# Two graph layers on one core: the table's scatters two rounds later, and the third graph sorted before its lists are made

## The reference

```python
scores = where(A != 0, -arange(N), -inf); vals, idx = top_k(scores, 25)
agg = X[idx].max(axis=2)                       # (N, 256) per graph
agg = where(degree <= 25, maximum(agg, 0), agg)
x1 = layernorm(X + relu(concat([X, agg]) @ W0 + b0))
Wh = x1 @ W1                                   # 8 heads of 32
e = leaky(s1[:, None] + s2[None, :] + edge_emb[1])   # per head
h = softmax(where(A == 0, -1e9, e)) @ Wh
out = layernorm(x1 + elu(layernorm(h) * gamma + beta))
```

## Time and profile before

| | before |
|---|---|
| median of three runs | 3414.9 us (3408.55 to 3415.16) |
| the profiled execution: its time | 3413.55 us |
| the profiled execution: its span | 3411.9 us |
| GpSimd (POOL) busy | 2487.7 us, 73% |
| VectorE (DVE) busy | 2417.1 us, 71% |
| TensorE (PE) busy | 1586.7 us, 47% |
| ScalarE (ACT) busy | 1113.9 us, 33% |
| DMA, mean over the span | 179 GB/s |

### The profile page before, as it was taken

The page is one execution under the profiler, slowest core; times in us unless marked ns, Lnnn a source line. Parts: engine busy times, 40 slices in busy tenths (PEclk is TensorE's granted clock), DMA queues, the critical chain, the costliest instruction groups (busy, mean ns, idle before and its releaser), DMA issues.

```text
span 3411.9 us, 25547 instructions
## 1 busy us (share of the span) xinstructions
PE 1586.7 (47%) x5123; PEld 1178.9 (35%) x5131; DVE 2417.1 (71%) x5791; ACT 1113.9 (33%) x2307; POOL 2487.7 (73%) x2612
## 2 busy tenths in 40 slices
PE   0036355444555344643555345554555434566454
PEld 0024233333343233432333233343334323344342
DVE  8798787667776668867786778767786455566666
ACT  3224343323333234342443334222332212223234
POOL 2476777777777777777777777777777777777775
PEclk9976667766666666766667666666667666667776
DMA  6657776655656566675666666555544444444332
GB/s 234 213 195 235 256 273 198 214 183 190 202 194 225 169 202 195 212 232 176 213 208 203 216 189 217 167 182 152 166 131 115 124 114 116 117 119 117 108 106 72
DMA packets 221587, 610.01 MB, mean 179 GB/s; under 512 B 68849, under 2 KB 112882, under 8 KB 194802
## 3 DMA queue, kind: packets, MB, share of 16 engines
q0 software_dynamic: 122880, 342.62, 33.8%
q1 hardware_dynamic: 98546, 265.71, 22.8%
HBM read 555.19 MB, written 52.95 MB: 178 GB/s over the span
## 4 chain that ended last, share of the span: by engine, by line
POOL 66%; issue 22%; DVE 7%; DMA 1%; DVEq 1%; ACT 1%; PE 1%; SPq 0%; POOLq 0%; ACTq 0%
POOL ring L590 57%; POOL sorted_d L567 4%; POOL out_dram L616 4%; DVE cand L1022 2%; DVE agg L1145 2%; POOL table_d L609 1%; DVEq L983 1%; POOL pair_s L600 1%; DVE adj_h L1018 1%; DMA adj_i<-in_adj_dram 0%; DVE lists L1006 0%; DMA ring<-sorted_d,idx_cur 0%; PE lin_p L844 0%; DVE agg L1135 0%; DMA pair_s<-sorted_d,pair_cur 0%
## 5 line engine op out<-in xcount | busy, mean ns | idle before, releaser
L590 POOL DMA_INDIRECT ring<-table_d,idx_loc x1096 | 1047.6, 956 | 333.9 <-issue 333.3
L590 POOL DMA_INDIRECT ring<-sorted_d,idx_cur x685 | 659.5, 963 | 208.7 <-issue 208.4
L852 PE MATMUL score_p<-ident,x1k 128*128 128x128 f32 x256 | 81.3, 419 | 1411.8 <-ACT x_t L690 1407.9
L880 PE MATMUL att_p<-ring,ident 128*128 128x256 f32 (+1 forms) x2384 | 602.4, 411 | 138.6 <-DVE ring L1302 138.0
L1145 DVE TENSOR_REDUCE agg<-ring 128x256 f32<-128x2560 f32 (+9 forms) x120 | 453.5, 3779 | 267.9 <-DMA ring<-sorted_d,idx_cur 183.6
L880 PEld LDWEIGHTS att_p<-ring,ident 128*128 128x128 f32 (+1 forms) x2384 | 497.4, 210 | 242.0 <-DVE ring L1302 126.7
L852 PEld LDWEIGHTS score_p<-ident,x1k 128*128 128x128 f32 x256 | 35.9, 197 | 1461.1 <-issue 1456.4
L721 ACT ACTIVATE neg<-z 128x256 f32<-128x256 f32 x128 | 53.3, 416 | 1466.9 <-DVE z L1188 1466.9
L590 POOL DMA_INDIRECT ring<-in_x_dram,idx_cur x411 | 395.3, 962 | 130.8 <-issue 124.3
L844 PE MATMUL lin_p<-w_s,h_t 128*128 128x256 f32 x1024 | 475.3, 645 | 0.0
L844 PEld LDWEIGHTS lin_p<-w_s,h_t 128*128 128x128 f32 x1024 | 319.9, 327 | 149.0 <-issue 80.9
(11 more groups left out here) (159 smaller groups left out, 2733.8 us busy)
## 6 DMA issues: line engine op xcount, KB each, us to landing
adj_i<-in_adj_dram SPq DMA_DIRECT2D x208, 1024.0 KB, 5.5
ring<-table_d,idx_loc POOLq DMA_INDIRECT x1096, 2.8
pay<-in_x_dram SPq DMA_DIRECT2D x8, 2048.0 KB, 9.9
xs<-sorted_d SPq DMA_DIRECT2D x128, 128.0 KB, 5.6
ring<-sorted_d,idx_cur POOLq DMA_INDIRECT x685
table_d<-tab SPq DMA_DIRECT2D x80, 132.0 KB, 3.9
ring<-in_x_dram,idx_cur POOLq DMA_INDIRECT x411
sorted_d<-pay,rank_i POOLq DMA_INDIRECT x128, 2.7
```

The source lines that it names most:

```text
L590: pool.indirect_dma_start(out=to[:, k * width:(k + 1) * width], out_offset=None, in_=source, in_offset=bass.IndirectOffsetOnAxis(ap=idx_at ...
L880: last = pe.matmul(att_p[:, 0:C], ident[0:on, :], r3[0:on, s, 0:C], start=(s == 0), stop=(s == k - 1))
```

## The change

`LAG0` goes from 7 to 9: the table's tile i is scattered in round i + 9, but at the latest in round 23 after its graph's first, so tiles 14 and 15 both come there, just ahead of the first gather of the graph's table. `RANKED` goes from 3 to 2: graph 2 is treated as graphs 3 to 7 were. Its 16 degree passes are put into `CASTS`: one behind each of the searches 19 to 23 in the prologue, two behind each search of rounds 0 to 4, one in round 5. Its sort thereby moves from round 25 to round 7, ahead of graph 1's in round 9. The later degree passes stand where they were. The prologue of SP and ACT is as long as the casts now ahead of round 0 (`CASTS_BEFORE` = 29, before 24).

```diff
-LAG0 = 7
+LAG0 = 9
-RANKED = 3
+RANKED = 2
 def order_casts():
-    order = [("search", n) for n in range(AHEAD + 2)]
+    first = iter(range(RANKED * T, RANKED * T + T))
+    order = []
+    for n in range(AHEAD + 2):
+        order.append(("search", n))
+        if n >= AHEAD - 3:
+            order.append(("degree", next(first)))
+    before = len(order)
     of_round = []
     for r in range(ROUNDS):
         start = len(order)
         if r + AHEAD + 2 < TILES:
             order.append(("search", r + AHEAD + 2))
-        if RANKED * T <= r + DAHEAD < TILES:
+        for n in [n for n in (next(first, None), next(first, None)) if n is not None]:
+            order.append(("degree", n))
+        if RANKED * T + T <= r + DAHEAD < TILES:
             order.append(("degree", r + DAHEAD))
         of_round.append(range(start, len(order)))
-    return order, of_round
+    return order, before, of_round
+def tables_in(r):
+    return [i for i in range(RANKED * T) if r == min(i + LAG0, i - i % T + LATER)]
 # SP's prologue
-            for n in range(T + 4, AHEAD + 4):
+            for n in range(T + 4, CASTS_BEFORE + 2):
                 load_adj(n)
 # GpSimd's round
-                if first(r - LAG0) and (r - LAG0) // T < RANKED:
-                    scatter_table(r - LAG0)
+                for i in tables_in(r):
+                    scatter_table(i)
 # ACT's prologue
-            for n in range(T, AHEAD + 2):
+            for n in range(T, CASTS_BEFORE):
                 cast(n)
```

More of the change, by code:

```diff
@@ L91, in order_casts @@
             order.append(("search", r + AHEAD + 2))
-        if RANKED * T <= r + DAHEAD < TILES:
+        for n in [n for n in (next(first, None), next(first, None)) if n is not None]:
+            order.append(("degree", n))
+        if RANKED * T + T <= r + DAHEAD < TILES:
             order.append(("degree", r + DAHEAD))
         of_round.append(range(start, len(order)))
-    return order, of_round
-CASTS, CASTS_OF = order_casts()
+    return order, before, of_round
+CASTS, CASTS_BEFORE, CASTS_OF = order_casts()
 CAST_AT = {c: k for k, c in enumerate(CASTS)}
+def tables_in(r):
+    return [i for i in range(RANKED * T) if r == min(i + LAG0, i - i % T + LATER)]
 def sorted_in(r):
```

## The result

| | before | changed | ratio, 95% interval |
|---|---|---|---|
| 15 runs each, first session: median | 3417.14 us | 3423.27 us | 1.0014 (1.0008 to 1.0021) |
| 11 runs against 15, a later session | 3409.56 us | 3411.19 us | 1.0006 (0.9997 to 1.0015) |
| profiled execution, first session: time (span) | 3413.55 us (3411.9) | 3415.21 us (3413.5) | |
| share of GpSimd's time busy | 73% | 72% | |

Forecast was 3401 us, 13 less than before. The changed kernel is 3 to 7 us slower in the first session and not to be told from before in the second. Twenty microseconds of work left the queue that bounds the kernel, and all of it came back as waiting.

A forecast was written before the change was run, and what follows sets the result against it. GpSimd's full queue, its indirect DMAs plus waits, was taken as the bound. Lists later +3.3, fewer scatters -18.2, a wait gone -2.4, landings +4: -13.3 us, so 3401 us; range 3391 to 3415.

The forecast's parts named there:

- Theory Q: Theory of the follow-up runs: GpSimd's queue, its count of DMAs plus its waits, explains the time; ratios named per run.
- Part 1: GpSimd's queue: graph 2's 16 table scatters become plain stores on SP's queue, 20.8 us less; gathers cost the same.
- Part 2: GpSimd before graph 1's lists: later scatters turn waits for ACT's table into one wait for graph 1's ranks.
- Part 3 (a): VectorE: graph 2's sort, now ahead of graph 1's, makes graph 1's ranks 8.7 us later.
- Part 3 (b): Prologue and rounds 0 to 5: extra degree-pass loads make VectorE 9.1 us late, 8.1 of it in the prologue.
- L: Time in us of one 1 MB degree-pass load in the prologue and early rounds; the forecast took 6.2.
- rival B: Prologue and rounds 0 to 5: loads of 7.2 to 8.8 us, ranks 5 to 20 us later than forecast; chance 0.17.
- A: The forecast itself: loads of 5.5 to 7 us, landings near their median, 3396 to 3405 us; chance 0.50.
- The cover that I claimed for late VectorE: After the lists: VectorE, 14.5 us later relative to GpSimd, is covered by 24 us of its waits for gathers.
- Part 4: First table gather of graphs 0 and 1: it waits for the scatters' landing, about 2 us each, +4 in all.
- C: Rounds 0 to 4: loads set the end from 8.8 us per load on; 3425 us at 9.2; chance 0.10.
- E: First table gathers: two landing waits of 6.7 us each, +9, 3410 us; chance 0.11.

The follow-up runs named there:

- y1: The changed kernel with table tiles 14 and 15 scattered one round earlier (22, not 23): 3408.67 us, 0.9983 of the kernel before.
- y3: The kernel before with only the scatter lag raised to nine (RANKED stays 3, no extra loads): 3414.46 us, 1.0003 of the kernel before.
- y4: The changed kernel with LAG0 back at 7, graph 2 still ranked: 3415.24 us, 1.0008 of the kernel before.
- z1: The changed kernel itself, run again in a later session: 3411.19 us, 1.0006 of the kernel before.
- z2: The changed kernel with graph 2's degree passes placed where the DMA engines had room, tiles 14 and 15 still in round 23: 3398.05 us, 0.9958 of before.
- z3: The kernel before plus graph 2's 16 degree passes where the change makes them, sums unused: 3427.00 us, 1.0049 of the kernel before.
- z4: The kernel before with the lag of nine alone, tiles 14 and 15 scattered in round 22: 3396.02 us, 0.9958 of the kernel before.
- y2: The changed kernel with degree passes placed where the DMA engines had room, tiles 14 and 15 in round 22: 3389.26 us, 0.9928 of before.

## Why the prediction was wrong

**What bounds the kernel: right.** In the nine profiles of changed kernels at this speed, the start of the last output scatter follows from GpSimd's count and waits to within 1.5 us, once each execution's own mean duration of an indirect DMA is put in. That is bookkeeping; what tests Theory Q are the ratios that it named beforehand. Those for y1, y3, y4, z1, z2, z3 and z4 came out inside the ranges given; y2's was missed, by more gain than forecast.

**Part 1: right.** 16 scatters of 1.004 + 0.30 us went, and the gathers cost the same from either source.

**Part 2: right in kind.** The waits for ACT's table turned into one wait for graph 1's ranks, 18.65 us at 328.02 (forecast: some 25 at 325). It is shorter because three scatters still waited for ACT before it, 5.8 us in all, and a gather waited 4.1 for a ring place at 298.4. That ring wait was named as a sign of being wrong; ahead of the wait for ranks it cost nothing.

**Part 3 (a), the second sort: right in size.** From round 6 to graph 1's ranks it was 53.1 us before and 60.2 in the first profile (+7.1); in y1, y2, y4, z1 and z2 62.3 to 63.1 (+9 to +10). Forecast +8.7.

**Part 3 (b), the loads: the first term that was mis-sized.** I gave 9.1 us: 8.1 for the prologue and 1 for rounds 0 to 5. The prologue's was right in the first profile, 7.8 at tile 22, and 7.9 to 11.1 in the others. In the rounds it was 6.0 in the first profile and 2.9 to 7.9 in the others, against my 1; (b) as a whole was 14.0, 16.5, 18.1, 10.8 and 15.8 in the five profiles with this placement (changed, z1, y1, y4, z3). The step that failed is "I take 6.2 because it is of this stretch". One load was taken for all, and it wasn't of the rounds. It came from 154 to 160 us. The next ones in the same profile, issued at 162.22 and 165.93 with the DMA engines some 0.9 busy, took 8.2 and 8.1 us, and the kernel before's view of its loads from 150 to 170 us has:

```profile
adj_i<-in_adj_dram SPq DMA_DIRECT2D x4, 1024.0 KB, 7.2
```

In the changed kernel the casts from 245 to 260 follow each other at 4.8 us, so a buffer's cycle is 9.6 us and a load takes 7.5; the 12 loads issued from 203 to 258 us landed after 6.8 to 8.6. The choice had a hole too: I used the ceiling of 356 GB/s only to say that loads would not be faster, though I had worked out that the rounds would ask for 365. A demand above the ceiling is not "at the ceiling"; it makes each load slower until the round gives way: here loads landed after 8.1 and 7.6 us (medians) where they had taken 5.1 and 5.7, and a round took 13.1 us instead of 11.9. And the ceiling isn't one number: 0.98 busy at 382 GB/s, 0.95 at 332. Of the two figures of the Trainium skill that I weighed (DMA: Bandwidth & Descriptors, Bandwidth: 358 GB/s for a core whose pair streams, 425 measured on one large transfer) neither was met: 382 with one core alone lies above the first and below the second, and 332 with the engines 95% busy below both. L = 7.5 lies in the lower half of rival B (7.2 to 8.8). B's formula gives 17 with it throughout; with 6.1 for the prologue and 7.5 for the rounds it gives 7.9 + 6.6 = 14.5, against 14.0 measured. So on this term B came true at its near end, not A.

**The cover that I claimed for late VectorE: wrong by 2.9 us.** I asked whether VectorE would hold GpSimd by a ring place or by late gathers, and not through SP. SP issued the load of graph 1's idx_cur at 346.1 before and at 362.11 now, 7 us after the last of the lists had landed (354.71), because in its queue it stands behind adjacency loads that wait for ACT's casts. The last of those loads, issued at 361.74, waited for the cast at 359.71, which had itself waited 0.69 us for its own load; the search casts before it waited for VectorE, up to 7.3 us:

```profile
356.47 5.60 SPq L438 DMA_DIRECT2D adj_i<-in_adj_dram  x2
362.11 0.43 SPq L448 DMA_DIRECT2D idx_cur<-sorted_d  x1
```

GpSimd met that at 373.97 with a wait of 3.17 us. The change moves work past three queues; I had followed GpSimd's and ACT's and left out SP's. A slip without effect stands beside it: the last plain store of a graph is two rounds old at the first gather of its table, not three, and still costs no wait.

**Part 4, the landings: the second term that was mis-sized.** Forecast 2 us each, measured 4.55 and 5.68 above the usual gap, 3.7 to 6.5 in y3, z1 and z2. The view from which I took 3.1 us, start to landing, now reads for all 32 scatters:

```profile
DMA to landing us min/median/max: 2.5/4.0/7.9
```

Two things went into the gap that the median doesn't have. First, these landings are long. The second of the two scatters, started at 497.56, had its last engine's landing at 502.59 by the trace's semaphore events, 5.03 us after its start; in the other graph and in z1 and z2 4.2 to 6.9. It isn't the pair as such: in y2 the last two of three scatters in a row, at 476.13 and 477.42, landed after 2.5 us each. It goes with how busy the DMA engines are. Of the 36 scatters of the kernel before whose landing its trace has, those with the DMA engines less than 0.60 busy from start to landing landed after 2.5 to 3.1 us (14 of them), those with 0.79 busy and more after 4.2 to 7.7 (12). Second, the gather began 0.80 us after the landing, in all six cases of the changed kernel, z1 and z2 (502.59 and 503.39, 921.10 and 921.90, 507.02 and 507.82, 923.63 and 924.43, 494.29 and 495.08, 911.15 and 911.95). So such a wait is landing - 1.0 + 0.8, not landing - 1.0. The row with the answer was in reach: the longest landing in the earlier trace rows is 7.7, and I put the middle of the sum at the median though the stretch ahead of the first table gather is a full one (0.88 busy from 480 to 490 in the kernel before). The Trainium skill's rule (the same page, Latency and other measured facts: HBM latency 0.2 us on average, up to 2 at high load), which I had given a sentence and no weight in the sum, pointed the right way: it made the sum -9.

**The sum.** Against -13.3: (b) 4.9 more and (a) 1.6 less, together +3.2 at the lists in the first profile (+8.6 in z1), top_cur +2.9, the tables +6.2, longer indirect DMAs +1.5. That is 13.8 of the 15.0 by which the last scatter missed. The rest is open. The sign that spoke was the last one named: the time from the lists' start to the last scatter shrank by 4.9 us (3081.4 to 3076.5), not by 14 to 18, while the lists at 328.0 stayed short of the 335 that would have meant B or C.

**The spread between executions.** The changed kernel's runs lie 12.5 us apart (3414.88 to 3427.37; 11.1 before in that session) and 14.3 in z1 (7.0 before). Its profiled execution, 3415.2, is the second fastest of 15, with its lists at 328.0; the same code started them at 333.4 and 334.1 elsewhere. The loads alone don't make this spread: z3 has 2.9 us over five runs, y1 6.7 over 11. The kernels with the table's last scatters right ahead of its first gather spread most: besides the changed one y3, without the loads, 12.6 over 11, and z2 17.1 over five; z4 and y2, without these waits, 2.8 and 5.2 over five. y4, with neither, has 10.9 over 11, so this is a pattern and not a cause. Which wait is longer in the longer executions was not seen, since only single executions are profiled.

**What was mispriced in the chances.** A had 0.50 with L up to 7; B and E together 0.28, and they were treated as alternatives. They came together: B near its lower end, and waits of 4.85 and 5.98 us, between A's 2 and E's 6.7. Nothing in them excludes the other, as z2 and z3 show, each of which has one without the other. So beside each alone a rival with both was due, some +8 for the loads and +6 for the landings, which is no change. And 15 runs a side told 0.14% from nothing (1.0008 to 1.0021), where I had written that less than 0.2% couldn't be told.

## What to carry to other kernels

When the queue that bounds a kernel is relieved of waits, the next wait on it is set by another chain; work that the change adds to that chain (here loads that make VectorE late) must be priced as if it lay on the path. Extra transfers want the stretch where the DMA engines are idle, not the one just before their data is needed: the same 16 loads made VectorE 11 to 18 us late in one place and 1 to 2 in another. A load time read for a forecast should be that of all the loads of the stretch, at the demand that the change will make, not that of one. And a store whose readers stand right behind it in the same queue costs its whole landing; one piece of other work between them, here one tile's gathers (10 us in y1), made it free.

## What the runs showed of the hardware that I had not expected

- The rate at which the DMA engines are full isn't one number: 0.98 busy at 382 GB/s, 0.95 at 332, 0.93 at 323 within 110 us of one execution, with some 106 GB/s of gathers and scatters in each. Why wasn't found.
- The same scatter of 128 rows landed 2.5 to 3.1 us after its start with the DMA engines less than 0.60 busy, and 4.2 to 7.7 with them 0.79 busy and more.
- GpSimd, released by the landing of a table scatter's last part, began 0.80 us later in six of six cases, where a release by VectorE or ACT took 0.3. The gather stands behind waits for four semaphores there; whether they or the landing cost the 0.5 more wasn't tried.
- One chip ran the kernel before in 4073 us instead of 3415, with the same durations of VectorE's and GpSimd's instructions (the changed kernel's VectorE was busy 2414 us there and 2417 here) and pauses between them: 39 of up to 5 us before one line alone. The profile names no releaser for most of them. The cause was not looked for, and the ranking of the variants was another one there.
